# Where the last layer's variances are taken: from transposed states in the stack, or from states loaded back in the FFN

## What is computed

```python
def _mingru(x, Wz, bz, Wh, bh):
    z = jax.nn.sigmoid(jnp.einsum('bsi,hi->bsh', x, Wz) + bz)
    h_tilde = jnp.tanh(jnp.einsum('bsi,hi->bsh', x, Wh) + bh)
    return _linear_scan(jnp.clip(1.0 - z, CLAMP_LO, CLAMP_HI), z * h_tilde)

def _stack(x, Wz, bz, Wh, bh, gamma, beta):
    h = x
    for i in range(L):                       # L = 4
        h_new = _mingru(h, Wz[i], bz[i], Wh[i], bh[i])
        if i > 0:
            h_new = h_new + h
        h = _layernorm(h_new, gamma, beta)   # over the 512 features of a token
    return h
...
h_comb = jnp.concatenate([h_fwd, h_bwd], axis=-1)
x = x + jnp.einsum('bsi,hi->bsh', h_comb, fusion_W) + fusion_b
x = x + _L0_ffn_ref(_layernorm(x, axis=-1), ...)
```

## Time and profile before

| what | value |
|---|---|
| median of 3 runs | 1540.48 us (1540.29 to 1540.55) |
| the profiled execution | 1540.21 us |
| its span, from the first to the last instruction | 1538.4 us |
| PE busy | 1518.7 us, 99% of the span |
| DVE, ACT, POOL busy | 1307.8, 1021.6 and 829.6 us |
| granted TensorE clock | 1.00 of full speed |
| HBM read and written | 73.95 and 37.77 MB |

### The profile page before, as it was taken

One profiled execution on the slowest core, in us unless ns is written; L12 is line 12 of the kernel. 1 busy time (PEld: TensorE's weight loads), 2 busy tenths in 40 slices (PEclk: granted clock), 3 DMA queues, 4 the chain that ended last, 5 costly groups with the idle time before them and its releaser, 6 DMA issues.

```text
span 1538.4 us, 22933 instructions
## 1 busy us (share of the span) xinstructions
PE 1518.7 (99%) x7744; PEld 1202.7 (78%) x7744; DVE 1307.8 (85%) x2021; ACT 1021.6 (66%) x1688; POOL 829.6 (54%) x1013
## 2 busy tenths in 40 slices
PE   9999999999999999999999999999999999999999
PEld 7877888888888888888888877777777777777776
DVE  8998999999899989999888887786877777776786
ACT  7988789898687897787987444445454444444354
POOL 6766657578868678676788632331423333332331
PEclk9999999999999999999999999999999999999999
DMA  4211212321312112122044551030302020111000
GB/s 171 76 37 68 103 56 90 124 69 63 123 40 85 56 41 90 65 94 89 29 145 143 193 171 42 1 110 1 96 15 89 22 89 22 62 48 41 29 20 36
DMA packets 73157, 113.20 MB, mean 74 GB/s; under 512 B 5193, under 2 KB 37961, under 8 KB 69970
## 3 DMA queue, kind: packets, MB, share of 16 engines
q1 hardware_dynamic: 72754, 111.21, 21.3%
q10 hardware_dynamic: 288, 0.52, 0.1%
HBM read 73.95 MB, written 37.77 MB: 73 GB/s over the span
## 4 chain that ended last, share of the span: by engine, by line
PE 50%; DVE 2%; ACT 1%; issue 0%; POOL 0%; DVEq 0%; ACTq 0%; POOLq 0%
PE ps L639 15%; PE ps L620 14%; PE ps L572 11%; PE ps L499 6%; PE ps L519 1%; PE ps L585 1%; PE ps L533 1%; PE ps L649 1%; DVE bnp L1132 1%; PE ps L662 0%; ACT H L876 0%; DVE H L1120 0%; DVE yb L1112 0%; ACT AH L880 0%; DVE H L1121 0%
## 5 line engine op out<-in xcount | busy, mean ns | idle before, releaser
L499 PE MATMUL ps<-AH,WH 128*128 128x512 f32 x896 | 366.9, 409 | 7.8 <-DVE H L1121 6.1
L499 PE MATMUL ps<-AL,WH 128*128 128x512 f32 x896 | 351.0, 392 | 0.0
L499 PE MATMUL ps<-AH,WL 128*128 128x512 f32 x896 | 349.4, 390 | 0.0
L1587 POOL TENSOR_TENSOR H<-H,yb 128x512 f32<-128x512 f32 x192 | 245.9, 1291 | 8.5 <-DVE yb L1112 1.3
L1112 DVE TENSOR_TENSOR_SCAN yb<-ab,ps 128x512 f32<-128x512 f32 x192 | 231.9, 1208 | 15.5 <-POOL ab L1578 9.1
L950 ACT ACTIVATE g<-ps 128x512 f32<-128x512 f32 x128 | 76.5, 598 | 248.7 <-PE ps L620 248.7
L837 ACT ACTIVATE yb<-ps,ncnd 128x512 f32<-128x512 f32 x224 | 158.2, 706 | 87.3 <-PE ps L499 84.2
L499 PEld LDWEIGHTS ps<-AH,WH 128*128 128x128 f32 x896 | 168.5, 188 | 46.3 <-DVE H L1121 8.6
L1307 DVE SCALAR_TENSOR_TENSOR gl<-g,wbcol,gh 128x512 fp32r<-128x512 f32 x118 | 116.9, 991 | 97.7 <-ACT gh L960 97.6
L499 PEld LDWEIGHTS ps<-AL,WH 128*128 128x128 f32 x896 | 168.1, 188 | 37.1
L1688 POOL TENSOR_TENSOR rs<-mv,nhalf 128x1 f32<-128x1 f32 x32 | 43.0, 1342 | 282.2 <-DVE mv L1279 282.2
(11 more groups left out here) (193 smaller groups left out, 3230.4 us busy)
## 6 DMA issues: line engine op xcount, KB each, us to landing
hs_scratch<-H SPq DMA_DIRECT2D x16, 1024.0 KB, 5.4
hc<-hs_scratch SPq DMA_DIRECT2D x32, 512.0 KB, 4.4
xr<-in_x SPq DMA_DIRECT2D x32, 256.0 KB, 4.5
out<-ob SPq DMA_DIRECT2D x32, 256.0 KB, 2.2
xbuf<-in_x SPq DMA_DIRECT2D x7, 1024.0 KB, 7.6
RAW<-in_wt SPq DMA_DIRECT2D x16, 256.0 KB, 6.3
stg<-in_fct SPq DMA_DIRECT2D x16, 256.0 KB, 3.2
stg<-in_pjt SPq DMA_DIRECT2D x16, 256.0 KB, 2.9
```

The costliest lines, as they stand in the source:

```text
L499: r = e.matmul(GATE[i % 3][:], w[:, q, m * 128:(m + 1) * 128], a[:, q, :], start=(n == 0), stop=(n == 11))
L1587: e.tensor_tensor(H[s][:, m, :], H[s][:, m, :], yb[i % 5][:], ALU.add).then_inc(s_v, 1)
```

## The change

The variances of the last layer are no longer taken in the stack for batches 1 to 6. Batch 0 and batch 7 stay as they were. `turned(t)` says which tails are still turned; for the others `tokens`, `stats` and `inv` return at once, in both directions, and their 96 banks leave the PSUM ring. For units 4 to 27 (`LATE` is 28) the FFN takes the variance from `hc` instead:

- `state_squares` on ScalarE squares the unit's states, 1024 elements to a partition;
- `state_sums` on GpSimd adds the four feature blocks of each direction to one, in two additions (512 and 256 elements), once for the states and once for the squares;
- `spread` on TensorE turns the four blocks that are left (4 transposes, into `TURNED`);
- `factors` on VectorE sums over 128 elements and forms the variance from mean square and squared mean in four small instructions;
- `state_factors` on GpSimd raises it to the power -1/2 into `rl`.

The states' load becomes `load_states`, issued one unit further ahead than the rows' (`load_rows`), since the sums need the states earlier. New buffers lie over `glx`, which only batch 7 uses.

```diff
+LATE = NU - 4
+def squared_at(b, c):
+    u = 4 * b + {1: 5, 4: 6, 7: 7, 13: 8}.get(c, 4 * NB)
+    return u if u < LATE else None
+def added_at(b, c):
+    u = 4 * b + {2: 5, 5: 6, 8: 7, 14: 8}.get(c, 4 * NB)
+    return u if u < LATE else None
+def spread_at(b, c):
+    u = 4 * b + {(0 if b > 0 else 1): 4, 4: 5, 7: 6, 10: 7}.get(c, 4 * NB)
+    return u if u < LATE else None
...
+def turned(t):
+    return t[2] < 3 or t[0] in (0, NB - 1)
...
         def tokens(tau, pr):
-            if tau is None:
+            if tau is None or not turned(TAILS[tau]):
                 return
...
+        def spread(u):
+            b, n = (u - 4) // 4, u - 4
+            e.wait_ge(f_hs, 4 * n + 4)
...
+            for k in range(4):
+                r = e.transpose(TURNED[:, k * 128:(k + 1) * 128], hsum[:, k, :], ident[:])
+            r.then_inc(f_ht, 1)
...
         for j in range(NB * NC):
             b, c = j // NC, j % NC
             fc(j)
+            if spread_at(b, c) is not None:
+                spread(spread_at(b, c))
...
+        def state_squares(u):
+            i, n = u % 2, u - 4
+            e.wait_ge(d_hc[i], 16 * (u // 2) + 16)
+            if n == 0:
+                e.wait_ge(d_hs[3], 64)
+            else:
+                e.wait_ge(f_hs, 4 * n - 1)
+            e.activation(hsq[:], hc[i][:], ACT.Square).then_inc(f_hq, 1)
...
             if b >= 2 and m == 0:
                 e.wait_ge(d_hs[s], stored((b - 2, 0, 3)))
                 e.wait_ge(d_hs[s + 1], stored((b - 2, 1, 3)))
-                e.wait_ge(s_t1, max(T1N[("T", TAIL[(b - 2, i, 3)], p, 1)] for i in (0, 1) for p in (0, 1)) + 1)
+                if b == 2:
+                    e.wait_ge(s_t1, max(T1N[("T", TAIL[(0, i, 3)], p, 1)] for i in (0, 1) for p in (0, 1)) + 1)
...
+        def factors(u):
+            n, r = u - 4, u % 2
+            e.wait_ge(f_ht, n + 1)
+            e.reduce_sum(htot[:, r, :], TURNED[:].rearrange("p (k n) -> p k n", k=4), axis=AX_X).then_inc(f_hr, 1)
...
             if h == 0:
-                if t == 0:
+                if 4 <= u < LATE:
+                    e.wait_ge(f_rl, u - 3)
+                elif t == 0:
                     e.wait_ge(s_rs, max(INVS[("h", TAIL[(b, d, 3)], p)] for d in (0, 1) for p in (0, 1)))
...
+        def state_sums(u, of_squares):
+            n, k = u - 4, 4 * (u - 4) + 2 * of_squares
+            src = (hsq if of_squares else hc[u % 2])[:].rearrange("p (d q) t -> p d q t", d=2)
...
+            e.tensor_tensor(pair, src[:, :, 0:2, :], src[:, :, 2:4, :], ALU.add).then_inc(f_hs, 1)
...
+            e.tensor_tensor(hsum[:, 2 * of_squares:2 * of_squares + 2, :], pair[:, :, 0, :], pair[:, :, 1, :],
+                            ALU.add).then_inc(f_hs, 1)
...
         addx(4)
+        state_sums(4, 0)
+        state_sums(4, 1)
...
+        def load_states(u):
...
+            if u >= 6:
+                e.wait_ge(f_hq, min(u - 5, LATE - 4))
+                e.wait_ge(f_hs, min(4 * (u - 6) + 1, 4 * (LATE - 4)))
...
         load_unit(4)
+        load_states(5)
         for u in range(NU):
             if u == 2:
                 spread_sums()
-            if u + 5 < NU and u + 5 > 4:
-                load_unit(u + 5)
+            if u + 6 < NU:
+                load_states(u + 6)
+            if u + 5 < NU:
+                load_rows(u + 5)
             if u >= 4:
                 store_out(u - 4)
```

More of the change, by code:

```diff
@@ L172 @@
         _i = subject(_who, _s - _o)
-        if _i is not None and _what == "T":
-            USERS += [("T", _i, _n, 0), ("T", _i, _n, 1)]
+        if _what == "T":
+            USERS += [] if _i is None or not turned(TAILS[_i]) else [("T", _i, _n, 0), ("T", _i, _n, 1)]
         elif _i is not None and (_who == "x" or TAILS[_i][2] < 3):
@@ L188 @@
 LOWS = {u: n + 1 for n, u in enumerate(u for u in order(START_LOW, LOW_SLOT) if layer(u) < 3)}
-STATS = {u: n + 1 for n, u in enumerate(order(START_STAT, STAT_SLOT) + [("h", LAST, 0), ("h", LAST, 1)])}
-INVS = {u: n + 1 for n, u in enumerate(order(START_INV, INV_SLOT) + [("h", LAST, 0), ("h", LAST, 1)])}
+STATS = {u: n + 1 for n, u in enumerate([u for u in order(START_STAT, STAT_SLOT) if turned(TAILS[u[1]])]
+                                         + [("h", LAST, 0), ("h", LAST, 1)])}
+INVS = {u: n + 1 for n, u in enumerate([u for u in order(START_INV, INV_SLOT) if turned(TAILS[u[1]])]
+                                        + [("h", LAST, 0), ("h", LAST, 1)])}
 SHIFTS = {u: n + 1 for n, u in enumerate(u for u in INVS if layer(u) < 3)}
@@ L308, in pixart_block @@
     sg = sb(p2, "sg", [128, 2, 4])
-    sb(p2, "pad", [128, 336])
+    htot = sb(p2, "htot", [128, 2, 4])
+    hmean = sb(p2, "hmean", [128, 2, 2])
+    hvar = sb(p2, "hvar", [128, 2, 2])
+    hve = sb(p2, "hve", [128, 2, 2])
+    sb(p2, "pad", [128, 304])
     x18 = sb(p2, "x18", [128, 512])
@@ L325, in pixart_block @@
     xh.append(sb(p2, "xh1", [128, KC, S], F32R))
-    glx = sb(p2, "glx", [128, 4, S], F32R)
+    with ExitStack() as p4:
+        glx = sb(p4, "glx", [128, 4, S], F32R)
+    with ExitStack() as p5:
+        hsq = sb(p5, "hsq", [128, 8, 128])
+        hpair = sb(p5, "hpair", [128, 4, 128])
+        hsum = sb(p5, "hsum", [128, 4, 128])
+    sb(p2, "under", [128, 4, S])
     gh = [sb(p2, f"gh{i}", [128, S], F32R) for i in range(3)]
@@ L390, in pixart_block @@
     f_rd = sem("f_rd")
+    f_hq, f_hs, f_ht, f_hr, f_hm, f_he, f_hv, f_rl = (
+        sem(n) for n in ("f_hq", "f_hs", "f_ht", "f_hr", "f_hm", "f_he", "f_hv", "f_rl"))
     f_ma, f_mp = sem("f_ma"), sem("f_mp")
@@ L586, in feat @@
             r.then_inc(f_t1, 1)
+        def spread(u):
+            b, n = (u - 4) // 4, u - 4
+            e.wait_ge(f_hs, 4 * n + 4)
+            if n % 4 == 0:
+                e.wait_ge(f_xh, u)
+                e.wait_ge(f_xl, u)
+            elif n % 4 == 1 and b > 0:
+                e.wait_ge(f_rd, 2 * b - 1)
+            elif n % 4 == 1:
+                e.wait_ge(f_hr, n)
+            else:
+                e.wait_ge(f_xh, u - 1)
+                e.wait_ge(f_xl, u - 1)
+            for k in range(4):
+                r = e.transpose(TURNED[:, k * 128:(k + 1) * 128], hsum[:, k, :], ident[:])
+            r.then_inc(f_ht, 1)
         def fc_of_first(t):
@@ L1078, in _ @@
         whole(4)
+        state_squares(4)
         for j in range(NB * NC):
@@ L1081, in _ @@
             hidden(j)
+            if squared_at(b, c) is not None:
+                state_squares(squared_at(b, c))
             if b > 0 and c == 2:
@@ L1529, in _ @@
             low_part(j)
+            if spread_at(b, c) is not None:
+                factors(spread_at(b, c))
             if b > 0 and c == 1:
@@ L1683, in addx, with state_factors @@
             e.tensor_tensor(xr[i][:], xr[i][:], fbb[:], ALU.add).then_inc(f_xf, 1)
+        def state_sums(u, of_squares):
+            n, k = u - 4, 4 * (u - 4) + 2 * of_squares
+            src = (hsq if of_squares else hc[u % 2])[:].rearrange("p (d q) t -> p d q t", d=2)
+            pair = hpair[:].rearrange("p (d q) t -> p d q t", d=2)
+            if of_squares:
+                e.wait_ge(f_hq, n + 1)
+            else:
+                e.wait_ge(d_hc[u % 2], 16 * (u // 2) + 16)
+                if n == 0:
+                    e.wait_ge(d_hs[3], 64)
+            e.wait_ge(f_hs, k)
+            e.tensor_tensor(pair, src[:, :, 0:2, :], src[:, :, 2:4, :], ALU.add).then_inc(f_hs, 1)
+            e.wait_ge(f_hs, k + 1)
+            if n > 0 and not of_squares:
+                e.wait_ge(f_ht, n)
+            e.tensor_tensor(hsum[:, 2 * of_squares:2 * of_squares + 2, :], pair[:, :, 0, :], pair[:, :, 1, :],
+                            ALU.add).then_inc(f_hs, 1)
+        def state_factors(u):
+            n, r = u - 4, u % 2
+            e.wait_ge(f_hv, n + 1)
+            e.tensor_tensor(rl[:, u // 4, :, u % 4], hvar[:, r, :], nhalf[:, 0:2], ALU.pow).then_inc(f_rl, 1)
         def inv_1(u):
@@ L1803, in _ @@
                 inv_2(b - 1)
+            if spread_at(b, c) is not None:
+                state_factors(spread_at(b, c))
+            if added_at(b, c) is not None:
+                state_sums(added_at(b, c), 0)
+            if c > 0 and added_at(b, c - 1) is not None:
+                state_sums(added_at(b, c - 1), 1)
             if j in (4, 7):
@@ L1915, in load_unit @@
             e.dma_start(xr[u % 3][:], x[b, q * 128:(q + 1) * 128, :]).then_inc(d_xr[u % 3], 16)
+        def load_unit(u):
+            load_states(u)
+            load_rows(u)
         for i in (0, 2):
```

18 lines of the change are left out of this document (17 added, 1 removed).

## The result

The changed kernel is slower: 1569.15 us median of 4 runs (1567.35 to 1569.42) against 1540.51 us (1540.29 to 1540.70) of the kernel before, ratio 1.0183, 95% interval 1.0166 to 1.0201. The forecast was 1538.6 us.

The account below looks back on a forecast made before the run. TensorE was taken to bound stack and FFN, VectorE close behind in the stack; 1540.21 - 21.0 + 0.5 + 10.3 + 7.4 - 1.0 + 1.7 + 0.2 = 1538.3, plus 0.27 for the median: 1538.6 us, range 1534.0 to 1543.5.

Parts of the forecast that it names:

- A call of `tokens` costs 0.87 us: Stack: each of 24 removed calls, 8 transposes each, frees 0.87 us of TensorE, -21.0 us in all.
- +0.5, between -1 and +3: Stack: ScalarE gets nothing back, so its sigmoid and tanh cost some tenths in two or three places, +0.5 us.
- the third rival: Stack: ScalarE and its chain set the pace, so -10.5 us instead of -21.0, total 1549.1 us; chance 0.07.
- Transposes of `spread`, 0.43: FFN: four new transposes on TensorE cost 0.43 us a unit, +10.3 us over 24 units.
- It has the cover: 5.35 us: FFN: VectorE's new work, some 1.2 us a unit, stays hidden by 5.35 us before `gelu` overwrites a buffer.
- The second rival: FFN: GpSimd's additions slow VectorE's instructions, 5.6 us against 5.35 of cover, +6, 1544.6 us; chance 0.10.
- The first wait: FFN's start: TensorE waits at `spread(4)` for GpSimd's additions, +7.4 us; the old wait for `resid(4, 0)` goes, -1.0.
- The clock behind it, 1.7: FFN's start: TensorE's granted clock falls during that wait and coming back costs +1.7 us.
- SyncE's order: FFN's start: later loads of `spread_sums` delay unit 6's additions and `spread(6)`, priced 0 to 1.5 us, taken as 0.2.
- the wait at the first new transposes: Sign at the FFN's start: TensorE's wait there names GpSimd's `hsum` and lasts 6 to 9 us.
- the stack's end: Sign: the stack ends 20 to 21.5 us sooner.
- the periods: Sign in the FFN: from one `moments` to the next takes 1.7 us more in six batches.

Follow-up runs that it names:

- e7: The changed kernel with batch 1 turned in the stack too and `resid(u, 0)` moved ahead of `total(j)` on VectorE: 1535.30 us.
- e8: As e7, with the four additions of a unit (`state_sums`) on VectorE instead of GpSimd: 1534.47 us.
- e12: As e8, with ScalarE's preparation of the FFN's weights behind `ntok` in three slots: 1534.41 us, 0.9962 of the kernel before.
- e1: The changed kernel, but from unit 5 on GpSimd's four additions cover one token instead of 128: 1545.59 us.
- e3: The changed kernel with one line moved on VectorE, `resid(u, 0)` ahead of `total(j)` and `squares(j)`: 1551.01 us.
- e10: The changed kernel with the loads of `spread_sums` one step sooner in SyncE's queue, ahead of `load_states(7)`: 1562.17 us.

## Why the prediction was wrong

- **A call of `tokens` costs 0.87 us: right.** 24 x 0.87 = 20.9, less the three waits of 5.4 and 0.6 us by which all of TensorE's rows are late from the start (60.94 for 60.32), is the 14.9 measured. Where the 0.6 comes from is open; e7, e8 and e12 don't have it.
- **"+0.5, between -1 and +3", ScalarE in the stack: mis-sized, 5.4.** The place was named, and rows without a gap were there to be followed. TensorE came 1.7 us sooner and ScalarE by nothing, so nearly all of it is lost, in three places. "Half of the stack's gain", the third rival, did not come.
- **Transposes of `spread`, 0.43: right.** e1's period is 84.87, 1.87 above before, for 4 x 0.43 = 1.72.
- **"It has the cover: 5.35 us": the step that failed, 19.1 us.** It was measured to `gelu`. The nearest reader of that stretch of VectorE's queue is `fuse(u, 1)` behind `resid(u, 0)`, with 2.4 us of cover, and VectorE came 4.55 us later. The second rival had the mechanism (GpSimd's additions slow VectorE's instructions down) and a price of the right size (5.6 us a unit). It was called unlikely, 0.10, only because of that cover, and set against it gave 0.25 us a unit. e1 shows that it is the additions, e3 that it is this one reader.
- **The first wait, 7.4 with -1.0 for the old one: right**, 6.9, and the old one is gone.
- **The clock behind it, 1.7: right in kind**, 2.2 by the spacing of the matmuls behind it. That the size nearly fits is in part luck: the first 28 transposes, from which the 1.7 was taken, take 4.75 to 6.16 us from run to run. The prediction missed that waits of 2 and 4 us lower the clock as well. Its sum without the term would be 1536.6, not 1536.4.
- **SyncE's order, "I take 0.2": mis-sized, 5.0 (e10).** The chain was written down right (loads, `whole_row(0)`, unit 6's additions, `spread(6)`); its lateness was guessed instead of added up.

Of the signs that it gave, the wait at the first new transposes (6 to 9 us) came, and the stack's end, the periods and `spread(6)` (3.9 us instead of under 1.5) were off. One of its signs of being wrong was met, waits in the stack grown by more than 3 us. The sign that it watched for VectorE was a wait for gelu, and none came: the wait was for `resid`.

## What to carry to other kernels

Cover is measured to the nearest reader of any instruction in the queue, not to the one that comes to mind: list all that stand behind the added work, with what waits for each. An addition that GpSimd makes beside a VectorE busy with two-input instructions is not free: here it cost VectorE what doing it would have cost (270.27 us busy with the additions on GpSimd, 268.51 with them on VectorE). Moving one awaited instruction ahead of the slowed ones bought back 18.1 us (e3), and in the periods as much as leaving the additions out (e1). Before a saving is booked on the busiest engine, look at each place whether the next engine's queue has a gap to follow into.

## What the runs showed of the hardware

A wait of TensorE can lower its granted clock to 0.50 to 0.56 (1.2 GHz) for the matmuls behind it, and one of about 2 us does so only sometimes. Over the changed kernel, the kernel before and all twelve experiments, from 100 us on, by the idle time in TensorE's rows and the granted clock of the 2.5 us behind it:

| idle time | waits | clock fell |
|---|---|---|
| 0.9 to 1.84 us | 120 | 0 |
| 1.92 to 1.96 us | 26 | 11 |
| 2.06 to 6.9 us | 14 | 14 |

The middle row holds the same wait in the same kernel, once with a dip and once without. Behind the waits of about 2 us a dip cost 1.7 us, nearly as much as the wait. One dip more or less would account for the 1.8 us by which one of this kernel's four runs was shorter; its mean clock was 0.995 for 0.993 in the others, but no trace shows where it gained.

An instruction of VectorE with two inputs of 512 elements in SBUF took 1.75 to 1.86 us instead of 0.68 to 0.74 where it ran beside one of GpSimd's additions of 512 elements, and 1.22 to 1.23 beside one of 256.
